# A sum moved from VectorE to TensorE and ScalarE, and one slot later, in the scan stage of a two-layer block

## The reference

```
def step(yt, wx_t):                       # layer 0, second half: a recurrence over the tokens
    yt = jax.nn.sigmoid(wx_t + yt @ Vt)
    return (yt, yt)
...
t = t + _L0_ffn_ref(_ln_t(t), ...)        # the residual of layer 0
...
forget_gate = jax.nn.sigmoid(x_ri @ Wf + bf + 2.0)      # layer 1, first half: per token
input_gate = jax.nn.sigmoid(x_ri @ Wi + bi)
delta = jax.nn.softplus(x_ri @ Wd + bd) * 0.1
... 16 steps of h = fg * (A h) + inp, written in closed form by the kernel
x = x + _L1_conv_ref(_ln_c(x), ...)       # the residual of layer 1: the sum that is moved
```

## Time and profile before

| | |
|---|---|
| median of 3 runs | 14604.2 us (14583.66 to 14649.89) |
| the profiled execution's own time | 14537.58 us |
| its span | 14535.8 us |
| scan stage with both scan and convolution, 22 chunks | 5684.4 to 11166.8 us |
| busy over the whole span: PE, DVE, ACT, POOL | 79%, 76%, 68%, 28% |

### The profile page before, as it was taken

The page is one execution under the profiler, slowest core; times in us unless marked ns, Lnnn a source line. Parts: engine busy times, 40 slices in busy tenths (PEclk is TensorE's granted clock), DMA queues, the critical chain, the costliest instruction groups (busy, mean ns, idle before and its releaser), DMA issues. The chain is left out here.

```text
span 14535.8 us, 248087 instructions
## 1 busy us (share of the span) xinstructions
PE 11419.5 (79%) x87538; PEld 8744.4 (60%) x87538; DVE 11053.6 (76%) x22880; ACT 9833.3 (68%) x22679; POOL 4012.8 (28%) x3975
## 2 busy tenths in 40 slices
PE   7888888888888867777777777777777547776998
PEld 5666666666666645555555555555555235555888
DVE  6777777777777718999999999999999965554133
ACT  6888888888888846666666666667666567776100
POOL 5444444445444421212111211112121111211000
PEclk9999999999999967777777777777777677777555
DMA  3333333333333321111111111111111133333599
GB/s 69 86 81 82 81 82 87 76 90 73 90 77 86 75 61 41 53 53 53 51 47 52 53 53 53 51 46 53 53 52 40 23 84 94 99 90 89 172 316 309
DMA packets 1967708, 1189.72 MB, mean 82 GB/s; under 512 B 48853, under 2 KB 1900056, under 8 KB 1958436
## 3 DMA queue, kind: packets, MB, share of 16 engines
q1 hardware_dynamic: 1554148, 967.87, 26.3%
q10 hardware_dynamic: 408832, 205.55, 5.0%
q0 software_dynamic: 3648, 2.20, 0.1%
HBM read 708.85 MB, written 466.62 MB: 81 GB/s over the span
## 5 line engine op out<-in xcount | busy, mean ns | idle before, releaser
L1236 PEld LDWEIGHTS s_pW<-s_XU,s_vh 128*128 128x128 f32 x6272 | 1415.7, 261 | 1969.1 <-ACT s_XU L1107 1699.7
L1236 PE MATMUL s_pW<-s_XU,s_vh 128*128 128x64 f32 x6272 | 1493.2, 331 | 1071.4 <-ACT s_XU L1107 1071.4
L1107 ACT ACTIVATE s_XU<-s_pW,s_zb 128x64 f32<-128x64 f32 x3136 | 995.7, 318 | 1788.7 <-PE s_pW L1236 1738.1
L1265 PE MATMUL s_pG<-s_wg,s_XNT 128*128 128x384 f32 (+1 forms) x3200 | 1506.0, 559 | 37.5 <-ACT s_Z L1086 37.5
L832 POOL TENSOR_TENSOR s_rst<-s_var,s_epst 128x16 f32<-128x16 f32 (+1 forms) x100 | 141.7, 1417 | 3906.6 <-DVE s_var L79 3906.6
L408 ACT ACTIVATE KB<-pV,qkb 32x392 f32<-32x392 f32 x2048 | 1190.5, 581 | 25.0 <-PE pV L498 1.1
L248 POOL TENSOR_TENSOR SS<-SS,mx 128x784 f32<-128x784 f32 x512 | 769.5, 1503 | 804.8 <-DVE mx L341 804.6
L1203 PEld LDWEIGHTS s_pY<-s_hident,s_XU 128*128 128x128 f32 (+1 forms) x3200 | 752.2, 305 | 177.7 <-issue 129.6
L1711 PE MATMUL c_pS<-c_OX,c_Wm 64*112 64x128 f32 x3584 | 737.6, 420 | 91.1 <-DVE c_X L1727 76.6
L460 ACT ACTIVATE XH<-XR,nm,rs 112x128 f32<-112x128 f32 x1792 | 733.6, 485 | 92.1 <-POOL nm L267 83.6
L506 PE MATMUL pS<-KB,QT 128*64 128x196 f32 x8192 | 793.7, 336 | 0.0
(11 more groups left out here) (249 smaller groups left out, 31958.3 us busy)
## 6 DMA issues: line engine op xcount, KB each, us to landing
XL<-in_x_dram SPq DMA_DIRECT2D x64, 1568.0 KB, 12.4
XR<-in_x_dram SPq DMA_DIRECT2D x64, 1568.0 KB, 18.0
x_dram<-XR SPq DMA_DIRECT2D x64, 1568.0 KB, 8.1
xh_dram<-XH SPq DMA_DIRECT2D x64, 1568.0 KB, 8.1
r_X<-x_dram SPq DMA_DIRECT2D x64, 1568.0 KB, 14.2
c_X<-x_dram SPq DMA_DIRECT2D x64, 1568.0 KB, 19.4
out_dram<-c_X ACTq DMA_DIRECT2D x64, 1568.0 KB, 13.9
s_XQ<-xh_dram ACTq DMA_DIRECT2D x384, 256.0 KB, 2.8
```

The costliest lines, as they stand in the source:

```text
L1107: act.activation(XU[j % 2][:, t, :], pW[t // R % 2][:, B * (t % R):B * (t % R) + B], ACT.Tanh, bias=zb[:, 0:1], scale=0.5).then_inc(u_sb, 1)
L1236: pe.matmul(pW[t // R % 2][:, B * (t % R):B * (t % R) + B], vh[:], before, start=False, stop=True, skip_group_check=True).then_inc(z_ps, 1)
L1265: pe.matmul(pG[i % 3][0:tc, 0:3 * C], XNT[:, i, 0:tc], wg[:], start=True, stop=True).then_inc(g_ps, 1)
```

## The change

The last VectorE instruction of a group (L1043, residual plus convolution) goes. L1041 loses its constant 0.5 and becomes a plain sum; it is now the last one, and `NV` is 23. Four pieces take the sum over, one slot later: for each quarter q of the group, PE adds the residual `X2` and `Wv` in bank `pN`, by two 512-column matmuls with the identity, and ACT evacuates the bank into `X2`, with the 0.5 as its bias. `slots()` yields a third group f = o - 1, and one slot more is appended at the end.

```
+            def last_sum(f, q):                                        # ACT, at k = 2, 4, 6, 8
+                act.wait_ge(f_ps, f * NQ + q + 1)
+                act.activation(X2[f % NX][0:tf_, Q * q:Q * q + Q, :]..., pN[0:tf_, :],
+                               ACT.Identity, bias=cols[0:tf_, 1:2]).then_inc(f_sb, 1)
...
+            def last_sum(f, q):                                        # PE, at k = 1, 3, 5, 7
+                wait(pe, f_sb, f * NQ + q)
+                pe.matmul(pN[0:tf_, :], ident[0:tf_, 0:tf_], X2[f % NX][...], start=True, stop=False, ...)
+                pe.matmul(pN[0:tf_, :], ident[0:tf_, 0:tf_], Wv[...], start=False, stop=True, ...).then_inc(f_ps, 1)
...
+                    if f is not None and k in (1, 3, 5, 7):
+                        if k == 1:
+                            pe.wait_ge(dv, f * NV + NV)
+                            ... wait(pe, n_sb, oc * NQ)
+                            if scan and s == NO - 2:
+                                pe.wait_ge(raw_d, j + 1)
+                        last_sum(f, k // 2)
                     if prep and k in (0, 3, 6, 9):
                         turn_inputs(j, s, k // 3, oc)
                     if conv and 11 <= k < 11 + NQ:
                         if k == 11:
...
+                            if f is not None:
+                                pe.wait_ge(f_sb, f * NQ + NQ)
...
-                    wait(dve, x3_st, o * 16)
...
                     after(7)
+                    wait(dve, f_ps, o * NQ)
                     turned_by(tm, Wv, inp, a, wp_d, wv_d, o)
...
-                    did(dve.scalar_tensor_tensor(flat(wv), flat(wv), 0.5, flat(inp), ALU.add, ALU.add))
-                    after(23)
-                    did(dve.tensor_tensor(flat(inp)..., X2[o % NX][0:tm]..., wv..., ALU.add))
+                    did(dve.tensor_tensor(flat(wv), flat(wv), flat(inp), ALU.add))
```

More of the change, by code:

```diff
@@ L641, in scan_phase @@
     HC = C // 2
-    NV = 24
+    NV = 23
     NA = 7
@@ L779, in load_x1 @@
                 c, s = divmod(o, NO)
-                wait(sp, dv, (o - NX + 1) * NV)
+                wait(sp, x3_st, (o - NX + 1) * 16)
                 sp.dma_start(X2[o % NX][0:size(c)], tokens(x1_d, OS * s, OS, c)).then_inc(x2_ld[o % NX], 16)
             load_x1(0)
-            for j, s, oc, o, scan, prep in slots():
-                if oc is not None and oc + 1 < NGR:
-                    load_x1(oc + 1)
+            for j, s, oc, o, f, scan, prep in slots():
                 if scan and s == 1:
@@ L790, in _ @@
                         sp.dma_start(D[:, at:at + e - a], dft[n, :, a:e]).then_inc(d_ld, 16)
[L791 to L796, removed]
+                if f is not None:
+                    c, s_ = divmod(f, NO)
+                    sp.wait_ge(f_sb, f * NQ + NQ)
+                    sp.dma_start(tokens(x3_d, OS * s_, OS, c), X2[f % NX][0:size(c)]).then_inc(x3_st, 16)
+                if oc is not None and oc + 1 < NGR:
+                    load_x1(oc + 1)
             sp.wait_ge(x3_st, NGR * 16)
@@ L1112, in _ @@
                         residual(oc + 1, (k - 25) // 2)
+                    if f is not None and k in (2, 4, 6, 8):
+                        last_sum(f, k // 2 - 1)
                     if prep and k in (1, 4, 7, 10):
@@ L1205, in turn_u @@
                 w.then_inc(y_ps, 1)
+            def last_sum(f, q):
+                c = f // NO
+                tf_ = size(c)
+                wait(pe, f_sb, f * NQ + q)
+                pe.matmul(pN[0:tf_, :], ident[0:tf_, 0:tf_], X2[f % NX][0:tf_, Q * q:Q * q + Q, :].rearrange("t b c -> t (b c)"),
+                          start=True, stop=False, skip_group_check=True)
+                pe.matmul(pN[0:tf_, :], ident[0:tf_, 0:tf_], Wv[0:tf_, :, Q * q:Q * q + Q, :].rearrange("t r b c -> t b r c"),
+                          start=False, stop=True, skip_group_check=True).then_inc(f_ps, 1)
             def turn_inputs(j, s, q, oc):
```

17 lines of the change are left out of this document (10 added, 7 removed).

## The result

The changed kernel takes 14989.9 us (median of 4 runs, 14952.06 to 15010.11) against 14607.5 us of the kernel before (median of 4 runs, three of them in the table above): ratio 1.0261, 95% interval 1.0243 to 1.0279. It is slower by 382 us. The profiled execution took 14971.17 us, with a span of 14969.4.

A forecast was written before the change was run, and what follows sets the result against it. The PE-ACT chain was taken as the bound in most of each chunk, VectorE elsewhere with 5.95 us to give; 22.0 us in 22 chunks (484) plus 13 made 497, forecasting 15101 us (3.4% slower), 8-in-10 range 14780 to 15480.

The forecast's parts named there:

- Three slots at 6.5 us: Slots s = 1, 2 and 3, step 1 to normalization: pairs and evacuations lengthen the PE-ACT chain by 6.5 us each.
- the fast bound: Slots s = 1 to 3: first pair at 1.2 GHz, all behind it at 2.4; 4.9 us per slot, 14964 us.
- one later pair would be slow: Slots s = 1 to 3: idle time between pairs may make one of the three later pairs slow again, 1.8 us.
- 600 to 700 as a sign: Matmuls into pN, profile after: mean 600 to 700 ns per instruction; near 590 clock fully back, near 1000 slow.
- The slot s = 0 at +2.5: Two pairs ahead of the last residual copy delay the normalization of s = 0 by 2.5 us, between 1.2 and 4.7.
- the rival in which the clock pays back: Clock stays at 2.4 GHz into the gates, taking 2.5 us per slot off the fast bound; 14773 us, chance 13%.
- What VectorE could give back: From BX of s = 2 to the statistics of s = 0: two instructions, 4.6 us per chunk, 101 us in all.
- VectorE's new wait: Wait for f_ps ahead of the first product into Wv: hidden before BX, costs nothing, with 3.5 us to spare.
- My sign of 4 to 7 us of wait at each BX: Profile after: VectorE would be busy under 90% and wait 4 to 7 us at each BX.
- The half chunk, the last one and the extra slot: Stretch after 11166.8 us: 18 us saved, paid back in waits for pairs and the added slot; 0, with 20 either way.
- The first chunk: Two slots of the first chunk cost 13 us together.
- the third rival: Clock gives back more than the pairs take, staying at 2.4 GHz into the gates; 14773 us, chance 13%.

The follow-up runs named there:

- e1: Kernel before without its last VectorE instruction, residual left out of the sum, nothing added on PE or ACT: 14587.3 us, ratio 0.9985.
- e2: Changed kernel with each of the eight matmuls of the sum cut to 64 columns from 512, evacuations and waits kept: 14717.3 us, ratio 1.0070.
- e7: Kernel before plus eight unread 512-column matmuls on PE at the head of slots s = 1 to 3: 14578.4 us, ratio 0.9988.
- e6: Changed kernel with pairs moved early into four banks, whole sum computed, plus e5's unread matmuls behind k = 12, 13, 14: 14465.6 us, ratio 0.9914.
- e11: e9 with e7's eight unread matmuls and e5's unread matmuls behind k = 12, 13, 14: 14605.1 us, ratio 1.0004.
- e5: e1 plus two unread 256-column matmuls on PE behind each of k = 12, 13 and 14, ahead of the gates: 14486.1 us, ratio 0.9922.
- e9: Changed kernel without pairs and evacuations; the whole sum is one 128x2048 GpSimd addition at the head of the next slot: 14659.2 us, ratio 1.0043.

## Why the prediction was right, and where not

The direction, the bound and the mechanism held: VectorE at 95% was not what the time hung on, and the pairs cost because they stand in the chain of scan steps (4.3 to 4.9 us in each of three slots). The size was 497 us in the profile's terms against 375 in the 22 chunks and 387 in the stage. By steps:

- Three slots at 6.5 us, between 4.9 (clock back behind the first pair) and 11.3. Measured 4.8, 4.9 and 4.3. This term was mis-sized by 5.5 us per chunk. The clock came back behind the first pair and did not fall again until 1.1 us ahead of the normalization at the earliest, so the fast bound was the right value, and its walk through steps and pairs was right to 0.2 us in s = 1 (18.66 us from step 1 to the normalization, worked out as 18.8). I had held that one later pair would be slow; none was. (The two matmuls of a pair have means of 742 and 670 ns per instruction, where I had named 600 to 700 as a sign; the first pair pulls them up.)
- The slot s = 0 at +2.5, between 1.2 and 4.7. Measured -0.3, below my bound. The last residual copy came 4 us later in its stretch, about as worked out (3.6). But from the statistics to the normalization it is 10.25 us (8115.67 to 8125.92), not the 12.1 that I carried over. The step that failed is the path: in the kernel after, the normalization of s = 0 no longer waits for GpSimd. GpSimd and ACT, after:

```profile
8119.86 0.22 POOL L830 TENSOR_TENSOR s_rst<-s_var,s_epst 128x16 f32<-128x16 f32 x1 [73.20 <-DVE s_var L79]
8120.16 2.91 POOL L832 TENSOR_TENSOR s_rst<-s_rst,s_nhalf 128x16 f32<-128x16 f32 x1
8123.15 0.73 POOL L834 TENSOR_TENSOR s_nmr<-s_mean,s_rst 128x16 f32<-128x16 f32 x1
```

```profile
8125.07 1.05 ACT L1063 COPY s_XU<-s_pX 128x512 f32<-128x512 f32 x1
8125.92 1.64 ACT L1126 ACTIVATE s_f<-s_X,s_nmr,s_rst 128x128 f32<-128x128 f32 x4
```

  GpSimd and VectorE, before:

```profile
8204.84 2.20 POOL L832 TENSOR_TENSOR s_rst<-s_var,s_epst 128x16 f32<-128x16 f32 x1 [63.74 <-DVE s_var L79]
8207.12 4.84 POOL L834 TENSOR_TENSOR s_rst<-s_rst,s_nhalf 128x16 f32<-128x16 f32 x1
```

```profile
8206.88 2.31 DVE L906 TENSOR_TENSOR s_Dl<-s_IN,s_par_a 128x2048 f32<-128x2048 f32 x1
```

  GpSimd's first two instructions take 3.1 us in place of 7.0. It is done at 8123.9, and ACT, with two more steps, a square and turned inputs ahead of it, gets to the normalization 2.0 us later. So the chain of steps and evacuations decides here too. It got 5.6 us longer (ACT would have been ready at 8206.8 before, 29.9 us behind the exponential, and takes 35.5 now), and the 5.95 us of slack paid for all of it. Before, VectorE ran its products beside GpSimd's instructions; after, it waits 1.7 us for a pair when they start. I had taken durations as fixed that depend on what the neighbour does.
- The gates: no term at all. Measured +3.4 us per chunk, 75 us in all. The gates stood only in the rival in which the clock pays back, and with the wrong sign.
- What VectorE could give back: I said 4.6 us per chunk and 101 us. e1 showed 3.7 in A and nothing in the period. The step that failed there is that the way from BX of s = 2 to the statistics would go on without a wait. It had none before, but BX of s = 3 stood only 0.2 us behind its normalization, so 1.3 us of the first instruction saved become a wait there in e1. What is left went to the later clock in B.
- VectorE's new wait: expected to cost nothing, by 3.5 us. It costs nothing, by 1.7 us, the wait that is left at BX. (My sign of 4 to 7 us of wait at each BX did not come true; that wait stands ahead of the first product instead.)
- The half chunk, the last one and the extra slot: 0 with 20 either way; measured 2.6 us (the stage behind 11166.8 before and 11551.2 after). The first chunk: 13, measured 9.8.

So part of the nearness is luck. The gates that I left out (+3.4 us per chunk) and the slot s = 0 that I set too high (by 2.8) nearly cancel, and what is left of the miss is the 5.5 us of the three slots. One sum in the prediction is wrong too: the third rival's 191 us over 14604 give 14795, not 14773.

The Trainium skill's rule that activity releases the throttle ("TensorE: Matmul & The Clock Gate", Part 1) would have given the fast bound, 4.9 us a slot, and 14964 us; the measured 14990 is nearer to that than to my 15101, though with the same two terms cancelling. The trace of the kernel after agrees with the rule in A, where the clock is 0.97 behind the first pair. The trace of the kernel before does not show it there, with a clock of 0.50 while PE is busy 10.8 of 13.9 us.

Left open: what decides at which gate the clock comes back. Kernels with the same matmuls in B differ by 5 us per chunk in it, and the changes that move it (e1, e2, e7) do nothing in B itself. That the cost of the change in B is the clock's is shown by the time at 1.2 GHz; why it is 3.4 and not 0 or 5 is not. The regular periods suggest that B fills the chunk up to the next step of 3.4 us, but no run varied A finely enough to test it. Why e6 and e11 gained less from the same matmuls than e5 was not followed up.

## What to carry to other kernels

Ask of added work in which wait it stands, not on which engine. The same eight matmuls per slot cost 17 us per chunk between the scan steps, with their evacuations. They cost nothing at the head of the slot, beside ACT's exponential (in s = 0, behind the residual's matmuls), in four banks, and there the clock is at its upper level over them.

A saving can be real in its own stretch and still not show, when another stretch takes it back. The cut alone showed 23 us and the clock alone 18, but both together 123, three times their sum, since the loss in the gates was paid once. Compare the stretches of a period and not only its length, and test two small savings together before either is dropped.

Do not read a group's mean as the duration of each. The 2.3 us of e9 were 1.2 in three slots and 5.6 in the fourth, and the fourth was the one on the chain.

## What the runs showed of the hardware that was not expected

- The granted clock turned a saving into nothing: e1 and the kernel before have the same period to 0.1 us, though A is 3.7 us shorter. Filling PE's short waits with six unread 256-column matmuls per slot, ahead of the gates, shortened B from 154.5 to 149.1 us per chunk, at a price of 2.0 in A.
- The periods of ten kernels whose chunks are all alike are 3.4 us or a multiple of it apart (245.8 to 266.2 us).
- GpSimd's durations depend on what VectorE is doing when they start. The power of 128x16 took 4.84 us when it started with 2.1 us left of a VectorE product (the rows before, above), 3.77 in s = 1 to 3 with 1.0 us left, and 2.91 with VectorE idle. In e2 it took 2.91 too, though a VectorE product started 0.05 us behind it and ran beside it. So what it lost is about what the running product still had to go. What holds it is not shown. e2:

```profile
8280.07 2.91 POOL L832 TENSOR_TENSOR s_rst<-s_rst,s_nhalf 128x16 f32<-128x16 f32 x1
```

```profile
8280.12 2.31 DVE L903 TENSOR_TENSOR s_Wv<-s_IN,s_par_a 128x2048 f32<-128x2048 f32 x1 [0.43 <-PE s_pN L1216]
```

- It holds in the other direction as well. A 128x1024 sum on VectorE took 5.60 us in e9 when it started 0.01 us behind GpSimd's addition of 4.53 us, and 1.23 without it. Not every VectorE instruction is held so: the 16 statistics instructions of s = 1 (`BATCH_NORM_STATS2`) took 3.19 us together beside the same addition, and 3.19 us in the kernel before without it.
